# The causal mask of a row maxima pass: from TensorE's identity matmuls into VectorE's maxima

## What is computed

```python
x = x + 0.5 * ffn(layernorm(x))           # silu(x Wg^T) * (x Wu^T), 2048 hidden, then Wd
x = x + attn(layernorm(x))
x = x + 0.5 * ffn(layernorm(x))

# attn: q, k are brought to unit norm, every other head is rotated (RoPE)
logits = einsum('bshd,bthd->bhst', q, k) * q_gain
logits = where(causal, logits, finfo.min)
attn = softmax(logits); y = einsum('bhst,bthd->bshd', attn, v) @ w_out
```

## Time and profile before

| | us |
|---|---|
| median of 3 runs (3142.15 to 3144.73) | 3144.57 |
| span of the profiled execution | 3141.4 |
| PE busy (23744 matmuls) | 2873.6 (91%) |
| DVE busy | 1808.9 (58%) |
| ACT busy | 1225.9 (39%) |
| POOL busy | 401.2 (13%) |
| DVE, the maxima L738 (512) | 245.7 |

### The profile page before, as it was taken

The page is one execution under the profiler, slowest core; times in us unless marked ns, Lnnn a source line. Parts: engine busy times, 40 slices in busy tenths (PEclk is TensorE's granted clock), DMA queues, the critical chain, the costliest instruction groups (busy, mean ns, idle before and its releaser), DMA issues.

```text
span 3141.4 us, 60646 instructions
## 1 busy us (share of the span) xinstructions
PE 2873.6 (91%) x23744; PEld 2078.2 (66%) x23744; DVE 1808.9 (58%) x4252; ACT 1225.9 (39%) x2218; POOL 401.2 (13%) x438
## 2 busy tenths in 40 slices
PE   4796679999999989999899998999899998999999
PEld 3573357766676667766577666766677665776666
DVE  8645463477535674476634775356744766347743
ACT  5223442355223542255423552235422554235522
POOL 0102200211002200022002110022000220021100
PEclk8896679999999999999999999999999999999999
DMA  6000000000000000000000000000000000000000
GB/s 229 1 1 1 1 14 1 1 8 2 22 1 1 8 22 1 1 2 8 22 1 1 8 2 22 1 1 8 22 1 1 2 8 22 1 1 8 2 8 14
DMA packets 15546, 37.94 MB, mean 12 GB/s; under 512 B 1408, under 2 KB 1408, under 8 KB 14720
## 3 DMA queue, kind: packets, MB, share of 16 engines
q1 hardware_dynamic: 15232, 33.70, 3.0%
HBM read 25.31 MB, written 8.39 MB: 11 GB/s over the span
## 4 chain that ended last, share of the span: by engine, by line
PE 60%; issue 22%; DVE 9%; ACT 5%; POOL 3%; DMA 0%; DVEq 0%; ACTq 0%; POOLq 0%; SPq 0%
PE psum L826 18%; PE psum L827 18%; PE psum L828 18%; ACT arena L537 2%; DVE mneg L738 1%; PE psum L980 1%; ACT arena L533 1%; PE psum L871 1%; PE psum L932 1%; PE psum L936 1%; DVE arena L759 1%; DVE arena L683 1%; POOL rn L418 1%; DVE arena L718 1%; POOL arena L437 1%
## 5 line engine op out<-in xcount | busy, mean ns | idle before, releaser
L826 PE MATMUL psum<-arena,WG 128*128 128x256 f16 x2048 | 564.2, 275 | 25.5 <-issue 19.7
L827 PE MATMUL psum<-arena,WG 128*128 128x256 f16 x2048 | 564.2, 275 | 0.0
L828 PE MATMUL psum<-arena,WG 128*128 128x256 f16 x2048 | 564.1, 275 | 0.0
L826 PE MATMUL psum<-arena,WU 128*128 128x256 f16 x2048 | 561.1, 274 | 0.0
L827 PE MATMUL psum<-arena,WU 128*128 128x256 f16 x2048 | 561.1, 274 | 0.0
L828 PE MATMUL psum<-arena,WU 128*128 128x256 f16 x2048 | 561.0, 274 | 0.0
L688 DVE SCALAR_TENSOR_TENSOR arena<-arena,psum 128x256 f32<-128x256 f32 x512 | 213.7, 417 | 551.9 <-ACT arena L548 551.4
L548 ACT ACTIVATE arena<-psum,tscale 128x256 f32<-128x256 f32 x512 | 242.5, 474 | 670.0 <-PE psum L828 669.4
L826 PE MATMUL psum<-WD,arena 128*128 128x512 f16 x1024 | 389.4, 380 | 34.5 <-DVE arena L694 34.3
L828 PE MATMUL psum<-WD,arena 128*128 128x512 f16 x1024 | 388.6, 379 | 0.0
L827 PE MATMUL psum<-WD,arena 128*128 128x512 f16 x1024 | 388.6, 379 | 0.0
(11 more groups left out here) (143 smaller groups left out, 4749.5 us busy)
## 6 DMA issues: line engine op xcount, KB each, us to landing
arena<-in_L_attn_x SPq DMA_DIRECT2D x16, 512.0 KB, 3.9
out<-arena SPq DMA_DIRECT2D x16, 512.0 KB, 2.8
arena<-in_L_ffn_w_gate SPq DMA_DIRECT2D x4, 1024.0 KB, 9.2
arena<-in_L_ffn_w_up SPq DMA_DIRECT2D x4, 1024.0 KB, 9.3
WD<-in_L_ffn_w_down SPq DMA_DIRECT2D x4, 1024.0 KB, 11.6
arena<-in_L_attn_w_qkv SPq DMA_DIRECT2D x1, 3072.0 KB, 19.5
WQ<-in_L_attn_w_out SPq DMA_DIRECT2D x1, 1024.0 KB, 21.7
ropet<-rope_table SPq DMA_DIRECT2D x1, 128.0 KB, 2.3
```

What stands on the lines that cost most here:

```text
L826: T_.matmul(o, lhs(0), rhs(0), start=first, stop=False)
L827: T_.matmul(o, lhs(0), rhs(1), start=False, stop=False)
L828: return T_.matmul(o, lhs(1), rhs(0), start=False, stop=last)
```

## The change

The mask matmul L959 goes, with the bf16 identity that it read. `maskq` grows from 128 to 512 columns: zeros, with the causal triangle in the last 128. VectorE's maximum of a tile becomes one instruction with two tensor inputs, the scores in PSUM and the last w columns of `maskq`: it adds them, writes the sum over the scores in PSUM, and writes the maximum of the row as an accumulator to `mpos`. The sign of the maxima is now positive, and `maxima` multiplies by the negative factor. Ahead of each bank's instructions VectorE sets one column of `carrier` to zero. The mask matmul of the second product (L981) reads the fp16 identity. To make room in SBUF, several small buffers share space: `wmax`, `wrec`, `wscale` lie on `ss`, `ss2`, `rn`, and three scratch columns of the gain on `mpos` and `yrec`.

```diff
-    identb = sb("identb", P, BF16)
-    maskq = sb("maskq", P, BF16)
+    maskq = sb("maskq", S, BF16)
...
-            for m in (ident, ident16, identb, maskq, maskk):
+            for m in (ident, ident16, maskq, maskk):
...
-            for m in (ident, ident16, identb):
+            for m in (ident, ident16):
...
-            link(nc.gpsimd.affine_select(out=maskq[:, :], in_=maskq[:, :], compare_op=ALU.is_ge, fill=MASKED,
+            link(nc.gpsimd.affine_select(out=maskq[:, S - P:S], in_=maskq[:, S - P:S], compare_op=ALU.is_ge, fill=MASKED,
...
                         wait("s1_ps", 48, 3 * (hf * HH + h) + bank + 1)
+                        V_.memset(carrier[:, bank:bank + 1], 0.0)
                         for t in tiles:
-                            ins = V_.tensor_reduce(mnegv[:, t, h:h + 1], ps(0, QSEG[t], (t + 1) * P), AX_X, ALU.max, negate=True)
+                            w = (t + 1) * P
+                            ins = V_.tensor_tensor_reduce(out=ps(0, QSEG[t], w), in0=ps(0, QSEG[t], w), in1=maskq[:, S - w:S], scale=1.0, scalar=2 * MASKED,
+                                                          op0=ALU.add, op1=ALU.max, accum_out=mposv[:, t, h:h + 1])
                         ins.then_inc(s["smax_done"], 1)
...
-                    link(V_.tensor_scalar(mstv[:, :, :, 0], src, 2.0 ** -12, None, ALU.mult))
+                    link(V_.tensor_scalar(mstv[:, :, :, 0], src, -2.0 ** -12, None, ALU.mult))
...
-                            T_.matmul(ps(0, QSEG[t], w), QT[0:ST, h, t * P:(t + 1) * P], KT[0:ST, h, 0:w], start=True, stop=False)
-                            ins = T_.matmul(ps(0, QSEG[t] + t * P, P), identb[:, :], maskq[:, :], start=False, stop=True)
+                            ins = T_.matmul(ps(0, QSEG[t], w), QT[0:ST, h, t * P:(t + 1) * P], KT[0:ST, h, 0:w], start=True, stop=True)
...
-                            ins = T_.matmul(ps(0, KSEG[t], P), identb[:, :], maskk[:, :], start=False, stop=True)
+                            ins = T_.matmul(ps(0, KSEG[t], P), ident16[:, :], maskk[:, :], start=False, stop=True)
```

More of the change, by code:

```diff
@@ L123, in build @@
     ropev = ropet[:, :].rearrange("p (t c) -> p t c", t=TT)
-    gain = sb("gain", 5 * H, F32)
+    gain = sb("gain", 2 * H, F32)
     hscale = sb("hscale", H, F32)
-    wmax = sb("wmax", 32, F32)
     wpow = sb("wpow", 32, F32)
-    wrec = sb("wrec", 32, F32)
-    wscale = sb("wscale", 32, F32)
     tscale = sb("tscale", HC, F32)
@@ L146, in build @@
     rn = sb("rn", 4 * HH, F32)
-    mneg = sb("mneg", TT * HH, F32)
+    mpos = sb("mpos", TT * HH, F32)
+    wmax, wrec, wscale = ss, ss2, rn
     mst = sb("mst", TT * MR, F16)
@@ L590, in _ @@
             dve.wait_ge(s["c_in"], 32)
-            g0, g1, g2, g3, g4 = (gain[:, i * H:(i + 1) * H] for i in range(5))
+            g0, g4 = (gain[:, i * H:(i + 1) * H] for i in range(2))
+            g1, g2, g3 = mpos[:, 0:H], mpos[:, H:2 * H], yrec[:, 0:H]
             link(V_.tensor_scalar(g1.bitcast(I32), g0.bitcast(I32), 0x7FFFFFFF, None, ALU.bitwise_and))
@@ L716, in unit @@
                     wait("qs_done", 8, i + 1)
-                    link(V_.tensor_tensor(rn[:, 16 * b2:16 * b2 + HH], rn[:, 16 * b2:16 * b2 + HH], gain[:, 4 * H + hf * HH:4 * H + (hf + 1) * HH], ALU.mult))
+                    link(V_.tensor_tensor(rn[:, 16 * b2:16 * b2 + HH], rn[:, 16 * b2:16 * b2 + HH], gain[:, H + hf * HH:H + (hf + 1) * HH], ALU.mult))
                     V_.tensor_tensor(qn[b2].rearrange("p (h c) -> p h c", c=HD), qs[b2].rearrange("p (h c) -> p h c", c=HD),
@@ L729, in stack_out @@
                     V_.tensor_copy(KT[0:ST, :, t * P:(t + 1) * P], ps16(3)[0:ST, :].rearrange("p (h n) -> p h n", h=HH)).then_inc(s["kt_ev"], 1)
-                mnegv = mneg[:, :].rearrange("p (t h) -> p t h", t=TT)
+                mposv = mpos[:, :].rearrange("p (t h) -> p t h", t=TT)
                 mstv = mst[:, :].rearrange("p (t h c) -> p t h c", t=TT, c=2)
@@ L746, in maxima @@
                         wait("mt_ps", 4, k)
-                    src = mnegv[:, :, g * GH:(g + 1) * GH]
-                    link(V_.tensor_scalar(mstv[:, :, :, 0], src, 2.0 ** -12, None, ALU.mult))
-                    V_.scalar_tensor_tensor(out=mstv[:, :, :, 1], in0=src, scalar=2.0 ** -12, in1=mstv[:, :, :, 0], op0=ALU.mult, op1=ALU.subtract).then_inc(s["mst_done"], 1)
+                    src = mposv[:, :, g * GH:(g + 1) * GH]
+                    link(V_.tensor_scalar(mstv[:, :, :, 0], src, -2.0 ** -12, None, ALU.mult))
+                    V_.scalar_tensor_tensor(out=mstv[:, :, :, 1], in0=src, scalar=-2.0 ** -12, in1=mstv[:, :, :, 0], op0=ALU.mult, op1=ALU.subtract).then_inc(s["mst_done"], 1)
                 def max_rows(hf, g):
```

## The result

The changed kernel takes 3159.89 us (median of 4 runs, 3158.55 to 3161.40) against 3143.36 us before on the same chip (four runs, 3141.70 to 3144.73): a ratio of 1.0053, 95% interval 1.0038 to 1.0067. It is slower by 16.5 us, where 23.5 were forecast.

What follows compares the result with a forecast made beforehand. VectorE, not TensorE, was taken to set the end ahead of all 32 turns of the maxima. 12.6 + 5.9 + 2.8 + 2.2 = 23.5 us onto the profiled span of 3141.4 gave 3164.9, as median 3168; range 3143 to 3215.

Steps and rivals of the forecast that it cites:

- TensorE's saving: Dropped mask matmuls, 0.06 us each, 0.24 us per head: at most 30 us, only where TensorE sets the pace.
- the ring: Cycle of scores, exponentials, subtractions and down matmuls in a half's last four heads; its period was not to move.
- e: Growth of VectorE's maxima per head, three memsets plus four δ: 0.37 us, bounds 0 and 1.0.
- δ: Surcharge of the new VectorE instruction over the plain maximum: 0.07 us, bounds 0 and about 0.2.
- Place (a): First four heads of 14 halves, batches 1 to 7: TensorE's turn of the maxima 0.90 us later each, 12.6 us lost.
- Place (c): Last of a half's second four heads, ahead of the second turn: e added in full, 16 x 0.37 = 5.9 us.
- Place (b): Last four heads, mixed with the first's scores and exponentials: price 0; the ring grows only from e = 0.7.
- Place (d): Batch 0, without a second stream to fill gaps: 2.8 us at its two turns, 2.2 us in its mixed stretch.
- the third: Rival: the new instruction's surcharge is near or above its bound; at e = 1.0 92 us lost, 3237 us; chance 0.18.
- The second (hardly dearer): Rival: new instruction hardly dearer, memsets hidden; 3140 us at e = 0, 3147 at e = 0.10; chance 0.14.
- The first: Rival: TensorE sets the pace everywhere, 30 us saved, 3115 us; chance 0.04.
- The clock: Fourth rival: TensorE's clock falls to 1.2 GHz as idle grows to some 2.5 us, a few us per turn; chance 0.04.

Runs made afterwards that it cites:

- e1: The changed kernel with TensorE's mask matmuls of the maxima pass put back, so the mask is added twice: 3158.06 us, ratio 1.0046.
- e2: The kernel before without the mask matmuls of the maxima pass, its own maxima taken over all keys of a tile: 3143.55 us, ratio 0.9999.
- e10: The kernel before without the maxima pass's mask matmuls, mask left out, plus 128 already met waits at the head of TensorE's program: 3139.35 us, ratio 0.9985.
- e8: The changed kernel with one more plain maximum of 256 columns per head on VectorE: 3186.39 us, ratio 1.0136.
- e9: The changed kernel unaltered, run again later beside other kernels: 3158.42 us, ratio 1.0049.
- e5: The changed kernel with two already met waits behind each score product of the maxima pass, in the loop's body alone: 3160.75 us, ratio 1.0055.
- e7: The changed kernel with 128 already met waits (64 instructions) at the head of TensorE's program: 3153.27 us, ratio 1.0031.
- e14: The changed kernel with the same 128 waits as e7, on another chip: 3152.94 us, ratio 1.0029.
- e13: The changed kernel with 16 already met waits (8 instructions) at the head of TensorE's program: 3162.14 us in a single run.

## Why the prediction was right, and where it was wrong

**What bounds.** Right. In every kernel the turns waited for VectorE. TensorE's 512 matmuls could be put back (e1) or taken away alone (e2) without a change that the runs can tell, though in both the second stall hides some 4 us; with it out of the way (e10) they are worth 4 us of their 30.

**TensorE's saving.** 0.06 us per mask held: the ring's wait grew by 0.24 us per head. Where it went was right in the ring and not quite at the first turns: I had TensorE wait there for all of its 0.96 us. The wait at the turns reached 33.6 us, not 57. With the steps as measured, the forecast's own reckoning gives 22.5 + 14 x (0.96 + 0.28) + 14 x 0.23 = 43, without batch 0; the 10 us and more that are still missing are waited for earlier in the stretch, where TensorE meets banks that the maxima haven't freed (0.37 us at 1480.55; 29.1 us in all in the weight loads, 4.8 before). This changes where it waits, not the end. But it spoils a sign that the prediction had named: the wait grew by 11.1 us, less than 16, which was to mean e below 0.1, and e is 0.175.

**e, the term that was mis-sized.** 0.37 us forecast, 0.175 measured. δ was 0.034 and not 0.07: the accumulator's read is listed with 140 ns and nearly all of it is overlapped. A memset costs 0.013 and not 0.03. The step that failed is the price of δ, made of two rows of about 60 ns: both are durations or differences of durations, and the prediction itself had found four maxima in 1.59 us whose durations sum to 1.92.

**Place (a).** With e = 0.175 the sum's own formula, 1475.84 + 3e, gives 0.22 us per first turn, and 0.28 was measured; e2 gave −0.29 where −0.31 was worked out, and e8, by 1475.57 + 4e, 1.49 for 1.46. The formula holds within 0.06 us; the missing 0.05 is probably that of place (c). The term came out as 3.9 us for 12.6. **Place (c).** 0.23 per turn for 0.37; 0.05 more than e, as the split waits for the last read of the accumulator (1482.85 + 0.14, L749 at 1483.02). 3.2 us for 5.9 − 0.7 of batch 0. **Place (b).** 0 as forecast; its upper bound of 0.7 was too high (e8). **Place (d).** Batch 0 lost 3.1 us in the profile of the changed kernel and 2.2 in e9, for 5.0 plus its 0.7 of (c). As a whole it tests nothing: between kernels whose batch 0 is the same it varies by 3 to 4 us (6.0 to 6.3 in e5, e7 and e14), and nearly all of that is there by the first turn. But from the first turn of a half to its second, the delay against the kernel before grows steadily: by 0.76 to 0.78 us in all five, for 4 x 0.27 + 0.37 = 1.45 forecast. With the prices as measured the same formula gives 4 x (2 x 0.013 + 3 x 0.034) + 0.23 = 0.74. So here too the place was right and e mis-sized.

**What the sum left out.** The second stall behind the loop's branch, some 6 us. With e as measured the four places give about 10 us, which is what e7 and e14 show (9.4 and 9.1); the stall makes up the rest of 16.5. So 23.5 for 16.5 was two errors of opposite sign: 13 us too much on VectorE, 6 too little for the place of the code. That the total came as near as it did is luck. The direction is not: without the second stall the kernel is slower too (e7, e14). I had written that everything else "keeps its instruction count" or hides; dropping matmuls does change TensorE's instruction count, ahead of the loop too.

**The rivals.** (In the third, batch 0 is 8 + 6 by the prediction's own formula and not 8 + 7, which changes nothing.) The second (hardly dearer) was closer on e than the forecast: at e = 0.2 it said 10 us, and without the stall that is the time. The first and third are out. The clock: in the profile of the changed kernel it did not fall at the turns, where TensorE is idle for 0.86 to 0.94 us in the rows above and not for 2.5. It does fall to the lower level, 1.2 GHz, behind the loop's branch, in both kernels. Over some 20 us from there the granted clock (the third number from the end) averages 0.69 to 0.84 in the six turns of the kernel before and 0.74 in each of the changed kernel's, here the last turn of each:

```profile
2639.00:2659.00 20.00, 13.97 (x97) 10.05 (x97) 12.43 (x36) 4.44 (x9) 2.74 (x5) 0.84 0.12 31
...
2653.00:2673.00 20.00, 13.48 (x87) 9.90 (x85) 12.39 (x36) 4.54 (x9) 2.40 (x5) 0.74 0.09 31
```

Summed over the six turns the clock is at the lower level for some 55 us before and 61 in the changed kernel, so up to 3 of the 6 to 7 us that go with the second stall can be clock. No run parts the two.

## What to carry to other kernels

Before work is moved off the busiest engine, read what ends its waits: where each stretch ends in a wait for the engine that would take the work over, the move is paid there once per stretch and the saving turns into more waiting. Price an instruction by start-to-start times in a dense run of its neighbours, not by its duration; for a new one, don't add durations of its parts. And in a kernel with a loop, a changed number of instructions ahead of the loop can add microseconds at each turn, so compare the idle time behind the branch in both traces before explaining a small difference by the change itself. When you pad a program, count the padding in the trace and not in the source.

## What was not expected of the hardware

Behind the branch at the loop's end TensorE stood for 2.6 to 3.8 us in all kernels but e13, and for another 2 to 2.8 us in the five that dropped the mask matmuls and had nothing (or only a longer loop body) put in their place: the changed kernel, e9, e2, e5 and e8. 64 instructions at the head of the program took the second stall away, 8 merged both into one of 6.2 to 7 us. The Trainium skill (Runtime: NRT & Kernel Launch, section Instruction fetch mechanics) says that instructions are refilled in blocks of 256 and that a taken branch to code outside the window waits for it to be fetched. The traces agree with this as far as they go. The place of the loop's start decides, and less whole blocks of 256 it is 178 or 186 in all six kernels with the longer standing and 50, 114 or 242 in the eight others; a block that ends some 8 instructions behind 178 would put the second wait where it is seen. But the block's size is not shown: an edge anywhere between 4282 and 4338 instructions parts the kernels as well. What would settle it is the kernel before with 128 real instructions (256 waits) more ahead of its loop: 4530, by blocks of 256 the changed kernel's place. It was not run.

A one-column memset listed with 59 ns costs 13 ns in a dense stretch, and a 140 ns read of the accumulator costs about 34 ns, together with what else the new instruction adds.
